# The decays' causal mask in a gated delta rule kernel: from an added -30000 on TensorE to a product on GpSimd

## The reference

```
g = -exp(A_log) * softplus(x @ a_w.T + dt_bias)
def step(S, inp):                       # for each position t
    q_t, k_t, v_t, g_t, b_t = inp
    S = S * exp(g_t)
    delta = (v_t - k_t @ S) * b_t
    S = S + outer(k_t, delta)
    o_t = q_t @ S
```

## Time and profile before

| | |
|---|---|
| median of 3 runs | 3312.14 us (3300.42 to 3313.62) |
| the profiled execution, its own time | 3311.1 us |
| its span in the trace | 3309.2 us |
| PE busy | 3135.2 us, 95% |
| DVE busy | 2492.2 us, 75% |
| POOL busy | 1907.1 us, 58% |
| ACT busy | 1679.1 us, 51% |

### The profile page before, as it was taken

The page is one execution under the profiler, slowest core; times in us unless marked ns, Lnnn a source line. Parts: engine busy times, 40 slices in busy tenths (PEclk is TensorE's granted clock), DMA queues, the critical chain, the costliest instruction groups (busy, mean ns, idle before and its releaser), DMA issues.

```text
span 3309.2 us, 117505 instructions
## 1 busy us (share of the span) xinstructions
PE 3135.2 (95%) x45504; PEld 2216.1 (67%) x45504; DVE 2492.2 (75%) x5472; ACT 1679.1 (51%) x3338; POOL 1907.1 (58%) x2865
## 2 busy tenths in 40 slices
PE   5999999999999999999999999999999999999986
PEld 4676666666666666666766666666667666667664
DVE  6877777777777777777777777777777777777762
ACT  4544555544555544555445555445555455554452
POOL 4566555666555666556665556665556665556643
PEclk8999999999999999999999999999999999999997
DMA  3000000000000000000000000000000000000000
GB/s 119 9 21 21 5 18 21 21 21 14 12 18 21 21 21 6 17 21 21 21 21 5 18 21 21 21 14 9 21 21 21 21 9 15 21 21 21 15 6 18
DMA packets 34301, 64.95 MB, mean 20 GB/s; under 512 B 5360, under 2 KB 7152, under 8 KB 33776
## 3 DMA queue, kind: packets, MB, share of 16 engines
q1 hardware_dynamic: 29808, 52.13, 4.6%
q10 hardware_dynamic: 4096, 6.42, 0.6%
HBM read 41.76 MB, written 16.78 MB: 18 GB/s over the span
## 4 chain that ended last, share of the span: by engine, by line
PE 82%; DVE 12%; issue 4%; SPq 0%; POOL 0%; DVEq 0%; DMA 0%; ACT 0%; POOLq 0%
PE PS L1181 18%; PE PS L1137 14%; PE PS L1168 9%; PE PS L1169 9%; PE PS L1250 7%; PE PS L1390 7%; PE PS L1236 3%; PE PS L1315 3%; DVE arena L891 3%; DVE arena L978 2%; PE PS L1268 2%; DVE arena L378 2%; PE PS L1286 2%; DVE arena L998 1%; PE PS L1329 1%
## 5 line engine op out<-in xcount | busy, mean ns | idle before, releaser
L891 DVE SCALAR_TENSOR_TENSOR arena<-PS,sc,arena 128x256 f32<-128x256 f32 x2112 | 1007.0, 483 | 382.6 <-ACT arena L594 280.5
L1168 PE MATMUL PS<-xh,wgu 128*128 128x256 f32 x2816 | 860.6, 340 | 60.9 <-DVE arena L999 51.6
L594 ACT ACTIVATE arena<-PS,sc 128x256 f32<-128x256 f32 x704 | 333.1, 476 | 875.2 <-PE PS L1169 761.2
L1181 PE MATMUL PS<-wdn,inner 128*128 128x512 f32 x1408 | 689.4, 617 | 29.3 <-DVE inner L903 29.3
L1169 PE MATMUL PS<-xl,wgu 128*128 128x256 f32 x2816 | 695.3, 282 | 0.0
L1168 PEld LDWEIGHTS PS<-xh,wgu 128*128 128x128 f32 x2816 | 532.8, 189 | 167.9 <-issue 83.4
L496 POOL TENSOR_TENSOR arena<-arena,work 128x31 f32<-128x31 f32 (+15 forms) x992 | 548.1, 552 | 77.7
L1169 PEld LDWEIGHTS PS<-xl,wgu 128*128 128x128 f32 x2816 | 533.4, 189 | 83.2 <-issue 83.2
L492 POOL TENSOR_TENSOR work<-arena 128x31 f32<-128x31 f32 (+15 forms) x992 | 517.4, 522 | 100.3 <-DVE arena L978 13.2
L1137 PE MATMUL PS<-xnT,wqkv 128*128 128x256 f32 x2048 | 487.3, 389 | 6.3 <-ACT inner L574 6.3
L1137 PEld LDWEIGHTS PS<-xnT,wqkv 128*128 128x128 f32 x2048 | 380.9, 192 | 71.7 <-issue 13.6
(11 more groups left out here) (153 smaller groups left out, 4554.0 us busy)
## 6 DMA issues: line engine op xcount, KB each, us to landing
xt<-in_x SPq DMA_DIRECT2D x64, 256.0 KB, 3.2
obuf<-in_x SPq DMA_DIRECT2D x64, 256.0 KB, 2.7
out<-obuf SPq DMA_DIRECT2D x64, 256.0 KB, 2.0
wqkv<-in_wqkv ACTq DMA_DIRECT2D x1, 2048.0 KB, 14.5
arena<-in_gup ACTq DMA_DIRECT2D x2, 704.0 KB, 6.4
arena<-in_dns SPq DMA_DIRECT2D x1, 1408.0 KB, 11.7
wg<-in_wg ACTq DMA_DIRECT2D x1, 1024.0 KB, 20.6
wo<-in_wo ACTq DMA_DIRECT2D x1, 1024.0 KB, 17.1
```

The source lines that it names most:

```text
L594: eng.activation(fa[:, u % 4, :], PS[:, bank(u, 0), 0:NB * P], ACT.Copy, scale=sc[:, u % 2, KB * m:KB * m + 1]).then_inc(fa_scaled.sem, 1)
L891: eng.scalar_tensor_tensor(out=fa[:, u % 4, :], in0=PS[:, bank(u, k // 2), k % 2 * NB * P:][:, 0:NB * P], scalar=sc[:, u % 2, KB * m + k:K ...
L1168: eng.matmul(o, w, xh[:, k, :], start=True, stop=False)
L1181: ins = eng.matmul(PS[:, b, :], inner[:, m, b * P:(b + 1) * P], wdn[:, m, :], start=(m == 0), stop=(m == FM - 1))
```

## The change

The third matmul of `log_decay` goes, and with it `negm`, `identb` and the two VectorE instructions that made them at the start. The bank then holds 0 where j is later than i, and its exponential is 1. A new function, `masked_decays`, multiplies E by `tri` in place on GpSimd, one instruction for each b, between `keys_for_R` and `layer_norm_scale`. `gram_products` waits for these in place of the exponentials.

```diff
+        def masked_decays(eng, n):
+            for b in range(NB):
+                hold(eng, *decay_done.at(n, b + 1))
+                eng.tensor_tensor(E[:, b, :, :], E[:, b, :, :], tri[:, :].unsqueeze(1).broadcast_to([P, H, CH]),
+                                  ALU.mult).then_inc(e_masked.sem, 1)
...
                 keys_for_R(eng, t, n)
+                masked_decays(eng, n)
                 if more:
                     layer_norm_scale(eng, n.next())
...
-                eng.wait_ge(*decay_done.at(n, b + 1))
+                eng.wait_ge(*e_masked.at(n, b + 1))
...
-            eng.tensor_copy(identb[:, :], ident[:, :]).then_inc(consts_done.sem, 1)
-            eng.tensor_scalar(negm[:, :], tri[:, :], 1.0, 30000.0, ALU.subtract, ALU.mult).then_inc(consts_done.sem, 1)
...
                 for part in (gm, gml):
-                    eng.matmul(PS[:, 4 + b, :], laterR[:, :], part[:, b, :, :].rearrange("p h i -> p (h i)"),
-                               start=(part is gm), stop=False)
-                eng.matmul(PS[:, 4 + b, :], identb[:, :], negm[:, :].unsqueeze(1).broadcast_to([P, H, CH]),
-                           start=False, stop=True).then_inc(decay_out.sem, 1)
+                    ins = eng.matmul(PS[:, 4 + b, :], laterR[:, :], part[:, b, :, :].rearrange("p h i -> p (h i)"),
+                                     start=(part is gm), stop=(part is gml))
+                ins.then_inc(decay_out.sem, 1)
```

More of the change, by code:

```diff
@@ L114, in build @@
         tri = sb("tri", [P, CH])
-        negm = sb("negm", [P, CH], BF16)
         laterR = sb("laterR", [P, P], F32R)
-        identb = sb("identb", [P, P], BF16)
         bdmask = sb("bdmask", [P, PV])
@@ L234, in build @@
         decay_done = signal("decay_done", 2)
+        e_masked = signal("e_masked", 2)
         qksq_done = signal("qksq_done", 2)
@@ L1213, in decay_sums @@
                     eng.wait_ge(consts_loaded.sem, 16 * 12)
-                    eng.wait_ge(consts_done.sem, 7)
+                    eng.wait_ge(consts_done.sem, 5)
                 sums = PS[:, 6, 0:NB * (2 * H + NHALF * NC)].rearrange("p (b n) -> p b n", b=NB)
```

## The result

The changed kernel is slower. Its median is 3344.62 us (3338.62 to 3345.73, 4 runs) against 3312.88 us; the ratio is 1.0103, with a 95% interval of 1.0086 to 1.012. That is 31 to 34 us more, where 25 were forecast. The profiled execution took 3338.62 us, with a span of 3336.8 us, 27.6 us longer than before.

What follows compares the result with a forecast made beforehand. TensorE, busy 95% of the span and 82% of the chain, was taken as the bound. A 24 us stall, some 1.7 us in the last step, less 0.5 us at the start, gave +25.2 us: 3337 us, range 3311 to 3353.

Steps and rivals of the forecast that it cites:

- The matmuls that go: TensorE's `log_decay`: two matmuls fewer a step, 15 to 21 us of its own time, worth nothing on the path.
- the prediction's condition for the matmuls to show: At `turn_kqn(0)`: a `products(0)` that ends sooner, cover gone on both sides, would let the 15 to 21 us show.
- The products' own time: GpSimd's E times `tri`: 1.28 us each, 1.05 as lower end; 67 to 82 us in all, within its idle time.
- Turns with VectorE: In `state(1)`: GpSimd's products and VectorE's two-SBUF-operand instructions shut each other out in turn, making VectorE 1.7 us late.
- The stall: Second half of TensorE's `y_times_s(2)` waits for the late state: 0.8 us a step, 24 us over 30 steps.
- The last step: xl stands behind the masks and the L919 of b = 1 wait for it too: some 1.7 us more.
- The sum: Whole kernel: stall and last step less the start give +25.2 us, so 3337 us, 0.75% slower.
- The 0.5 us at the start: Start of kernel: 0.5 us off, once, for the two VectorE instructions removed and what the first tile may gain.
- No blocking: Rival: masks fit in GpSimd's idle time, VectorE not held, matmuls off the path; 3312 us, chance 0.10.
- the shorter block: Rival at `state(1)`: masks of 1.05 us or paired L919 give a 0.31 us stall; 3322 us, chance 0.20.
- Full worth for the matmuls: Rival: TensorE gets back 0.24 to 0.33 us for each removed matmul; 3291 to 3297 us, chance 0.06.
- A further stall at `y_times_s(3)`: Rival of more than one stall: late VectorE also misses `y_times_s(3)`, some 0.4 us more a step; 3349 us, chance 0.14.

Runs made afterwards that it cites:

- e1: The changed kernel without the products on GpSimd, E left unmasked; 0.9982 of the kernel before, 3318.13 us.
- e4: e3 with `keys_for_R` also moved on GpSimd, behind the late products; 0.9972 of the kernel before, 3310.91 us.
- e10: e4 with the first gate matmul moved on TensorE from behind `turn_kqn(0)` to between `log_decay(1)` and `k_times_u(1)`; 1.0003 of the kernel before, 3323.43 us.
- e3: The changed kernel with `masked_decays` moved on GpSimd from behind `keys_for_R` to behind `keys_for_state`; 0.9977 of the kernel before, 3320.02 us.
- e7: The changed kernel with each product of E and `tri` replaced by E times the constant 1.0, mask left out; 0.9986 of the kernel before, 3315.78 us.
- c0: The kernel before, unchanged, run as a control against itself; ratio 1.0001.
- e11: e5 with the first gate matmul moved as in e10, additive mask and its matmuls kept; 1.0019 of the kernel before, 3329.51 us.
- e5: The kernel before with `keys_for_R` moved on GpSimd behind `keys_for_state`, matmuls and additive mask kept; 0.9981 of the kernel before, 3314.11 us.
- e8: The changed kernel with the two products on VectorE, between `state(3)` and the first feed-forward unit; 0.9982 of the kernel before, 3317.98 us.
- e9: The changed kernel with only the product of b = 0, E of b = 1 left unmasked; 0.9971 of the kernel before, 3318.94 us.
- e2: The kernel before with `masked_decays` added on GpSimd and its third matmul kept; 1.0085 of the kernel before, 3352.69 us.

## Why the prediction was right, and where its size was off

**The matmuls that go: right, with the wait at the wrong place.** They were put at nothing, and e1 shows 2.77 us for the stretch against 2.78. But the prediction let the wait before `turn_kqn(0)` grow from 0.22 to 0.5 us as its sign. It is 0.22 us still. The time of the matmul of `log_decay(0)` went into the wait for `state(0)`, which grew from 0.18 to 0.37 us, and that of `log_decay(1)` into `k_times_u(1)`. That one waits for ScalarE's copy, a cover the prediction did not name ahead of the one it did. ScalarE's two copies for this chunk, after the change:

```profile
1568.56 1.07 ACT L620 ACTIVATE ub<-PS 32x512 f32<-32x512 f32 x2
```

They start as `y_times_s(1)` ends and take 1.07 us, while the two matmuls left in `log_decay(1)` end 0.46 us ahead of them (1568.77 + 0.40 against 1569.63). e4 and e10 bear it out: with `products(0)` early the matmul was still free, and 0.46 us of another matmul went in for nothing. So the prediction's condition for the matmuls to show, a `products(0)` that ends sooner, was too weak.

**The products' own time: right.** 1.28 us was taken over 1.05; e3 measured 1276 ns. The prediction passed over the rows of GpSimd that already multiply by `tri`, those of `masked_g`, which spoke for the lower price:

```profile
L442 POOL TENSOR_TENSOR xl<-gl,tri x64: 1038/1042/1049, 52.2 to 3152.9; 128x512 fp32r<-128x512 f32 x64
```

There the other operand is g, one value repeated over the 32 columns, as in the row of 1.05 us. So a `tri` repeated over the heads did not make the product with E cheap.

**Turns with VectorE: right, instruction by instruction.** Counted from `turn_kqn(0)`, `state(1)` was to end at 1563.86 - 1560.65 = 3.21 us, and does at 1573.59 + 0.48 - 1570.85 = 3.22. The products were to end 1562.95 - 1560.31 = 2.64 us behind the end of `keys_for_R`, and end 1573.14 - 1570.51 = 2.63 us behind it. The Trainium skill's "GPSIMD Engine Reference" (Key points) names VectorE's instructions with two SBUF inputs, and the trace agrees, 2.20 us against 0.48. That section does not say what e7 shows, that it also depends on GpSimd's instruction.

**The stall: right in kind, 0.07 us too small.** 0.8 was taken and 0.87 came. The second half was late by 3.37 - 2.59 = 0.78 us, where 0.77 was worked out. The rest is that the 16 matmuls of that half then took 0.52 us in place of 0.43, which the term had left out. It is not the stop as such: in `y_times_s(1)` 16 matmuls behind a like wait take 0.43. Its cause is open.

**The last step: right.** There xl blocks the second pair as well. After the change, VectorE and TensorE in that step:

```profile
3193.93 2.14 DVE L926 SCALAR_TENSOR_TENSOR S<-S,exs,tmp 128x64 f32<-128x64 f32 x2
```

```profile
3191.19 1.04 PE L1333 MATMUL PS<-ident,arena 128*128 128x128 f32 x4 [0.33 <-DVE arena L377]
...
3196.21 0.43 PE L1272 MATMUL PS<-S,YT 32*32 32x64 f32 x16 [0.61 <-DVE S L926]
```

5.02 us where the earlier trace rows have 3.42: 1.6 us, and 1.7 were forecast. The clock is low here too (`turn_kqn(0)` takes 1.04 us in place of 0.66), but the second half still waits 0.61 us for the state, so VectorE sets this time.

**The sum.** 30 x 0.87 + 1.6 = 27.7 us, and the span grew by 27.6. That these agree is luck. With the three steps at the lower clock the stretch gives 28.3 + 1.6 = 29.9 us, and all else in this pair of traces came out 2.3 us shorter. In c0 the kernel before has a span of 3319.1 us, 9.9 us more than in the trace shown, and none of it in the stretch. The term that was mis-sized is the stall. It explains 30 x 0.07 = 2.1 of the 6 to 9 us by which the medians differ more than forecast, and the steps at the lower clock, which the sum did not have, 2.2 us. The 0.5 us at the start can't be read off against such differences. The rest is not attributed. Steps differ in length within each of these traces by 2.2 us (the kernel before, 99.56 to 101.73 us) or more, partly by TensorE's clock. In the kernel before, TensorE stands idle for VectorE for 1.6 and 1.0 us late in each step, and some steps run on at a lower granted clock and others do not. The same place in two of them (length, TensorE's busy us, then its granted clock):

```profile
1589.00:1592.00 3.00, 2.79 (x18) 1.00 0.00 0
1689.00:1692.00 3.00, 3.00 (x12) 0.59 0.00 0
```

0.59 over 3 us is mostly the lower of the two levels.

**The rivals.** No blocking and the shorter block fell by the rows above. Full worth for the matmuls fell by e1 and e4. e11 shows when the one of `log_decay(1)` counts: with both covers gone. The one of `log_decay(0)` counted in no run. A further stall at `y_times_s(3)` did not come. VectorE's `state(2)` ends 1.31 us late, counted from `turn_kqn(0)`, where 1.4 was forecast, and so close that TensorE takes up `y_times_s(3)` 0.16 us behind it (1578.56 to 1578.72). xl ends 1.30 us late, and TensorE does not wait for it.

**A version that beats both.** e4, with the matmul gone, the masks and `keys_for_R` behind `keys_for_state`, is at 0.9972 of before, 3310.91 against 3321.62 us. By the rows, 30 x 0.29 = 9 of the 11 us are the 0.29 us a step of `keys_for_R`, which the kernel before can have without the change (e5). e4 and e5 themselves (0.9972 and 0.9981) are not told apart by their intervals.

The five kernels with the matmul out, no stall and `keys_for_R` where it was (e1, e3, e7, e8, e9) came out at 0.9971 to 0.9986, though the stretch shows no gain in e1. So the removal may be worth some 0.2% elsewhere in the step, but the runs do not agree on it. With the stall in place the kernel that keeps the matmuls (e2, 1.0085) is no slower than the one without (1.0093 and 1.0103). The traces show 0.04 us a step, 1 us in all: `y_times_s(2)` takes 0.65 us in e9 and 0.72 us before, and half of that is lost again right behind it. The rest is open.

## What to carry to other kernels

An idle engine is not a free engine: before work is put on GpSimd, look at what VectorE does in those microseconds. If it runs instructions with two SBUF operands, each can be held for a whole two-operand product of GpSimd (0.97 and 1.30 us here, in place of 0.28), and the same product some 15 us later is free. Work out such a collision as a sequence of turns up to the instruction that someone waits for, and compare it with the slack there; it is a threshold, not a proportion (one product 0, two products 0.87 us a step). And a matmul ahead of a wait is worth nothing on a TensorE that is 95% busy, until every wait behind it is filled.

## What was not expected of the hardware

- A one-operand instruction of GpSimd over 128x512 took 1.56 us on average, longer than the two-operand product (1.28 us), and held VectorE back by 0.43 us at most (e7).
- Moving one gate matmul by a few places brought TensorE an issue pause of 0.86 us inside `y_times_s(2)` in the step shown (e10), and such pauses, 0.74 us a step, cost more than the 0.46 us that the move won.
- Where the wait before `y_times_s(1)`'s second half is about 0.37 us, TensorE's granted clock fell to the lower level behind it in 8 of 270 steps, and where it is 0.18 us in none of 150. Four gate matmuls then took 3.20 us in place of 1.88 (after the change, step 4). That the one follows from the other is not shown.
